# Macaron kernel: the mixer's carry factors leave GpSimd for ScalarE and VectorE, under a new table of places for all jobs

## What is computed

```python
x = x + 0.5 * ffn(layernorm(x))      # passes q = 0..3, one for each batch
x = x + mixer(layernorm(x))          # mixers b = 0..3
x = x + 0.5 * ffn(layernorm(x))      # passes q = 4..7
```

```python
L = clip(cumsum(-dt in the chunk), -20, 0)
cum_decay = clip(cumsum(L[:, :, -1, :]), -80, 0)
ncd = clip(cum_decay - max(cum_decay), -20, 0)
carries = cumsum(shifted(bout * exp(-ncd))) * exp(ncd)
final = chunk_out + carries * exp(L)
```

## Time and profile before

| | before |
|---|---|
| median of 3 executions | 259.51 us (259.31 to 259.81) |
| the profiled execution | 260.13 us |
| its span in the trace | 258.3 us |
| TensorE busy | 251.7 us, 97% of the span |
| VectorE busy | 211.1 us, 82% |
| ScalarE busy | 195.1 us, 76% |
| GpSimd busy | 82.9 us, 32% |
| granted TensorE clock, mean share of full speed | 0.997 |

### The profile page before, as it was taken

How to read it: one execution, slowest core, us unless ns; L and a number is a source line. 1 busy time by engine, 2 the same in 40 slices (tenths; PEclk the granted TensorE clock), 3 DMA queues, 4 the chain that set the end, 5 groups by cost and what they waited for, 6 DMA issues and landing times.

```text
span 258.3 us, 4609 instructions
## 1 busy us (share of the span) xinstructions
PE 251.7 (97%) x1540; PEld 218.6 (85%) x1540; DVE 211.1 (82%) x536; ACT 195.1 (76%) x236; POOL 82.9 (32%) x90
## 2 busy tenths in 40 slices
PE   7999999999999999999999999999999999999994
PEld 7979999998998979899979999878678687887894
DVE  4656587798589799999999999999999998675712
ACT  1255664866999877968848989999989957979650
POOL 5225306920019700995502957500306002000000
PEclk9999999999999999999999999999999999999998
DMA  6589749855100077430700700700007000570022
GB/s 194 176 255 338 121 81 362 177 221 206 63 0 0 13 94 242 47 38 9 260 0 0 81 4 0 247 0 0 0 4 246 0 0 3 155 229 24 0 84 82
DMA packets 21975, 26.18 MB, mean 101 GB/s; under 512 B 1280, under 2 KB 17152, under 8 KB 21952
## 3 DMA queue, kind: packets, MB, share of 16 engines
...
...
## 4 chain that ended last, share of the span: by engine, by line
PE 91%; ACT 3%; issue 2%; DMA 1%; DVE 1%; POOL 0%; SPq 0%; DVEq 0%; ACTq 0%; POOLq 0%
PE hid_ps L845 32%; PE y_ps L873 28%; PE y_ps L898 10%; PE aux_ps L984 5%; PE aux_ps L940 4%; PE aux_ps L1016 3%; PE aux_ps L1005 3%; PE hid_ps L1023 2%; PE y_ps L917 1%; PE aux_ps L965 1%; ACT hid L639 1%; DMA m_tok<-wpack_dram 1%; ACT late L729 1%; PE y_ps L1028 1%; PE hid_ps L917 1%
## 5 line engine op out<-in xcount | busy, mean ns | idle before, releaser
L845 PE MATMUL hid_ps<-z_hi,w_parts 128*128 128x512 f32 x256 | 83.9, 410 | 0.4 <-ACT w_parts L592 0.4
L873 PEld LDWEIGHTS y_ps<-w_sb,hid 128*128 128x128 f32 x640 | 77.1, 192 | 4.3 <-DMA w_sb<-wpack_dram 0.8
L873 PE MATMUL y_ps<-w_sb,hid 128*128 128x128 f32 x640 | 78.1, 275 | 0.4 <-ACT hid L639 0.4
L639 ACT ACTIVATE hid<-hid_ps,w_sb 128x1024 f32<-128x1024 f32 x56 | 61.8, 1109 | 16.7 <-PE hid_ps L845 16.4
L845 PEld LDWEIGHTS hid_ps<-z_hi,w_parts 128*128 128x128 f32 x256 | 45.2, 189 | 9.5 <-issue 1.4
L845 PE MATMUL hid_ps<-z_lo,w_parts 128*128 128x512 f32 x128 | 40.1, 394 | 0.0
L1223 DVE TENSOR_TENSOR hid_lo<-hid,hid_hi 128x1024 fp32r<-128x1024 f32 x19 | 22.9, 1218 | 7.8 <-ACT hid_hi L646 7.8
L845 PEld LDWEIGHTS hid_ps<-z_lo,w_parts 128*128 128x128 f32 x128 | 24.0, 188 | 5.6
L646 ACT ACTIVATE hid_hi<-hid 128x1024 fp32r<-128x1024 f32 x19 | 19.6, 1054 | 1.3 <-PE y_ps L898 1.2
L486 POOL TENSOR_SCALAR bias_tok<-w_sb,coef 128x128 f32<-128x128 f32 x10 | 7.3, 734 | 39.1 <-DMA w_sb<-wpack_dram 25.2
L1110 DVE TENSOR_SCALAR f_tok<-xt,f_mv,f_rstd 128x128 f32<-128x128 f32 x64 | 17.7, 351 | 2.0 <-POOL f_rstd L464 1.9
...
## 6 DMA issues: line engine op xcount, KB each, us to landing
w_parts<-w_split SPq DMA_DIRECT2D x12, 512.0 KB, 4.1
w_split<-mix_tmp SPq DMA_DIRECT2D x8, 512.0 KB, 4.9
...
xt<-bias_tok POOLq DMA_DIRECT2D x5, 512.0 KB, 6.5
...
xt<-x_dram SPq DMA_DIRECT2D x3, 512.0 KB, 8.4
out_dram<-xt SPq DMA_DIRECT2D x3, 512.0 KB, 3.2
```

The lines of the kernel that those rows point to most:

```text
L639: nc.scalar.activation(hid[:, slot % HBUF, :], hid_ps[:, slot % 2, :], ACT.Gelu, bias=bias).then_inc(hid_ready, 1)
L845: last = nc.tensor.matmul(hid_ps[:, slot % 2, cols], w, z[:, q % 2, cols], start=first, stop=end)
L873: last = nc.tensor.matmul(y_ps[:, cols], hid[:, slot % HBUF, cols], w_sb[:, q % 2, k, W2_AT + f * P:W2_AT + (f + 1) * P], start=t == 0 and ...
```

## The change

GpSimd's three small jobs per mixer are gone. ScalarE takes the exp of the first decays straight from `decay` (a scale of -1 in the instruction), in an instruction of its own; VectorE computes `ncd` and the differences behind its scan of `cumd`. All tables of places are set anew.

```diff
     "dve": {
...
-        "m_scan2": {0: 930, 1: 1266, 2: 1631, 3: 1995},
+        "m_scan2": {0: 956, 1: 1244, 2: 1586, 3: 1992},
...
-            def mixer_carry_steps(b):
-
-                pool.wait_ge(cumd_done, b + 1)
-                if b:
-                    pool.wait_ge(small_exp, b)
-                nc.gpsimd.tensor_scalar(small[:, 0, :], first_of(decay), -1.0, None, ALU.mult).then_inc(first_done, 1)
-                nc.gpsimd.tensor_scalar(ncd[:, :], cumd[:, :], cumd[:, 0:1], DECAY_MAX,
-                                        ALU.subtract, ALU.min).then_inc(ncd_done, 1)
-                pool.wait_ge(ncd_done, b + 1)
-                nc.gpsimd.tensor_tensor(small[:, 1, 1:NCH], ncd[:, 0:NCH - 1], ncd[:, 1:NCH],
-                                        ALU.subtract).then_inc(small_done, 1)
...
                 nc.scalar.activation(alpha[:, :], dstep[:, :], ACT.Exp).then_inc(alpha_exp, 1)
-                act.wait_ge(first_done, b + 1)
+                act.wait_ge(decay_done, b + 1)
+                nc.scalar.activation(small_e[:, 0, :], first_of(decay), ACT.Exp, scale=-1.0).then_inc(first_exp, 1)
                 act.wait_ge(small_done, b + 1)
-                nc.scalar.activation(small_e[:, :, :], small[:, :, :], ACT.Exp).then_inc(small_exp, 1)
+                nc.scalar.activation(small_e[:, 1, :], small[:, :], ACT.Exp).then_inc(small_exp, 1)
...
                 V.tensor_tensor_scan(cumd[:, :], last_of(decay), cum_cap[:, :], 0.0,
                                      ALU.add, ALU.min).then_inc(cumd_done, 1)
+                dve.wait_ge(cumd_done, b + 1)
+                V.tensor_scalar(ncd[:, :], cumd[:, :], cumd[:, 0:1], DECAY_MAX,
+                                ALU.subtract, ALU.min).then_inc(ncd_done, 1)
+                dve.wait_ge(ncd_done, b + 1)
+                if b:
+                    dve.wait_ge(small_exp, b)
+                V.tensor_tensor(small[:, 1:NCH], ncd[:, 0:NCH - 1], ncd[:, 1:NCH],
+                                ALU.subtract).then_inc(small_done, 1)
```

More of the change, by code:

```diff
@@ L50 @@
     "pe": {
[L51 to L58, removed]
@@ L59 @@
-        "y_turn_y": {5: 2206, 6: 2426, 7: 2600},
+        "f_norm": {1: 169, 2: 349, 3: 809, 4: 1129, 5: 1509, 6: 1806, 7: 2166},
+        "f_route": {1: 189, 2: 529, 3: 869, 4: 1169, 5: 1529, 6: 1829, 7: 2186},
+        "m_norm": {0: 509, 1: 829, 2: 1209, 3: 1489},
+        "m_dt": {0: 669, 1: 1029, 2: 1349, 3: 1629},
+        "m_v": {0: 749, 1: 1069, 2: 1409, 3: 1669},
+        "m_gate": {0: 929, 1: 1269, 2: 1589, 3: 1926},
+        "m_heads": {0: 985, 1: 1309, 2: 1606, 3: 2046},
+        "m_out": {0: 992, 1: 1389, 2: 1612, 3: 2066},
@@ L81 @@
[L81 to L89, removed]
@@ L90 @@
-        "m_scan2": {0: 930, 1: 1266, 2: 1631, 3: 1995},
[L91 to L95, removed]
+        "c_proj": {0: 110},
@@ new lines @@
+        "f_route": {1: 330, 2: 576, 3: 884, 4: 1200, 5: 1573, 6: 1845, 7: 2203},
+        "f_split_w1": {1: 339},
+        "f_coef": {1: 528, 2: 687, 3: 974, 4: 1312, 5: 1611, 6: 1901, 7: 2279},
+        "f_bias": {5: 1988, 6: 2150, 7: 2533},
+        "m_stats": {0: 422, 1: 728, 2: 1042, 3: 1362},
+        "m_normalise": {0: 487, 1: 819, 2: 1160, 3: 1481},
+        "m_clip": {0: 536, 1: 862, 2: 1238, 3: 1529},
[3 rows of a table added]
+        "m_silu": {0: 633, 1: 977, 2: 1317, 3: 1619},
+        "m_silu_lo": {0: 656, 1: 993, 2: 1337, 3: 1629},
@@ new lines @@
+        "m_decay": {0: 747, 1: 1079, 2: 1380, 3: 1681},
+        "m_dstep": {0: 787, 1: 1131, 2: 1416, 3: 1824},
+        "m_cos": {0: 800, 1: 1119, 2: 1454, 3: 1773},
+        "m_sin": {0: 810, 1: 1148, 2: 1468, 3: 1832},
+        "m_u": {0: 835, 1: 1186, 2: 1495, 3: 1855},
+        "m_u2": {0: 870, 1: 1203, 2: 1517, 3: 1956},
+        "m_carry": {0: 904, 1: 1142, 2: 1425, 3: 1819},
+        "m_scan": {0: 925, 1: 1218, 2: 1536, 3: 1968},
+        "m_scan2": {0: 956, 1: 1244, 2: 1586, 3: 1992},
@@ L96 @@
+        "m_gated": {0: 984, 1: 1327, 2: 1614, 3: 2061},
+        "m_add": {0: 999, 1: 1406, 2: 1624, 3: 2076},
+        "s_lo": {40: 1739, 41: 1752, 42: 1810, 44: 1884, 45: 1923, 46: 1945, 48: 2052, 49: 2068, 50: 2124,
+            51: 2178, 52: 2191, 53: 2207, 54: 2287, 55: 2304, 56: 2322, 57: 2388, 58: 2420, 59: 2459, 60: 2482},
+        "y_update": {0: 405, 1: 711, 2: 1030, 3: 1348, 4: 1669, 5: 2371, 6: 2516, 7: 2584},
     },
     "act": {
-        "c_split_rest": {0: 19, 1: 60},
-        "c_pre_hi": {0: 170, 1: 180, 2: 190, 3: 300, 4: 413, 5: 448, 6: 456, 7: 464},
@@ L100 @@
[L100 to L114, removed]
+        "c_split_rest": {0: 60, 1: 100},
+        "c_pre_hi": {0: 250, 1: 260, 2: 270, 3: 293, 4: 453, 5: 466, 6: 497, 7: 508},
@@ new lines @@
+        "c_proj_hi": {0: 485},
+        "f_turn": {1: 180, 2: 340, 3: 813, 4: 1133, 5: 1493, 6: 1786, 7: 2150},
+        "f_split_w1": {1: 306},
+        "f_tanh": {1: 491, 2: 586, 3: 944, 4: 1226, 5: 1536, 6: 1866, 7: 2180},
+        "f_split_w2": {5: 1613, 6: 1968, 7: 2300},
+        "m_scale": {0: 502, 1: 826, 2: 1180, 3: 1460},
+        "m_tap": {0: 514, 1: 853, 2: 1213, 3: 1506},
+        "m_silu": {0: 573, 1: 936, 2: 1270, 3: 1552},
+        "m_silu_hi": {0: 620, 1: 952, 2: 1300, 3: 1580},
@@ L117 @@
     },
     "pool": {
[L119 to L123, removed]
+        "f_rstd": {1: 40, 2: 173, 3: 620, 4: 901, 5: 1449, 6: 1518, 7: 1812},
+        "f_bias": {0: 293, 1: 559, 2: 691, 3: 1049, 4: 1315},
+        "m_rms": {0: 452, 1: 757, 2: 1067, 3: 1381},
@@ L233, in macaron_kernel @@
         dt_t, decay, alpha, u = (mix_tmp[:, i, :] for i in range(PRE_BUF))
-        small = sb("small", [P, 2, NCH])
+        small = sb("small", [P, NCH])
         small_e = sb("small_e", [P, 2, NCH])
@@ L549, in _ @@
                     mixer_affine(b)
-                for b in placed(tick, at["m_carry"]):
-                    mixer_carry_steps(b)
         @block.scalar
```

48 lines of the change are left out of this document (24 added, 24 removed), and 6 rows, old and new, of the table AT.

## The result

The changed kernel takes 261.44 us (median of 5 runs, 261.08 to 261.85); the kernel before takes 259.36 in the same measurement (5 runs, 259.31 to 259.81). The ratio, taken from the single executions and not from the two medians (which would give 1.0080), is 1.0072, with a 95% interval of 1.0057 to 1.0087. The sign and the range of the forecast (260.8 us) held; the loss is 2.08 us by the medians where the sum said 1.34. One execution of all that follow, in e11, ran at a granted clock of 0.563 and took 424.58 us; its ratio leaves it out.

The account below looks back on a forecast made before the run. TensorE's waits were taken to set the time, with VectorE full from `m_gated(0)` to mixer 2's final scan. Loss 2.76 (0.6 + 0.4 + 1.76) less gain 1.42 gave +1.34: median 260.8 us, own range 259.9 to 262.0, overall 259.2 to 262.1.

Parts of the forecast that it names:

- TensorE's own work is unchanged, only waits count: TensorE, busy 251.7 of 258.3 us, keeps its work; the time can move only by what TensorE waits.
- Front 0.3: At `down(0)`: `gelu(0)` no longer stands behind a weight split that waited on a DMA; gain 0.3 us.
- Middle 0.26: At the `down` at 83.05: its gelu no longer stands behind mixer 0's decay block; gain 0.26 us.
- Late 0.86: Between `down(42)` and `down(43)`: nothing stands between `gelu(42)` and `gelu(43)` any more; gain 0.86 us.
- GpSimd's instructions cost nothing before: GpSimd's twelve carry instructions: ScalarE's exp over `small` never waited for them, so removing them gives nothing by itself.
- The added VectorE instructions, 0.22 each: Four added instructions in `m_carry(1)` and `m_carry(2)`: 0.22 us each, 0.88 in all, between 0.6 and 1.2.
- Up to `m_heads(2)`, 0.6 + 0.4 late: VectorE from `m_gated(0)` to mixer 2's final scan: 0.6 us late with hand-over, plus 0.4 new idle time.
- From there to `hid_lo` of slot 40, 1.76: Behind `m_heads(2)`: VectorE needs 16.70 us, TensorE 14.94; loss 1.76, showing at `m_out(2)` and `down(40)`.
- VectorE freed by an idle GpSimd: VectorE, no longer held by GpSimd, keeps up and only the gains stay: 258.1 us; chance 0.13.
- Loss and gain meet: The 0.6 and 0.4 may be nothing and the second stretch lose only 1.4: 259.5 us; chance 0.13.
- ScalarE late as well: `m_silu(3)` ahead of `gelu(38)` delays `down(38)`, or pass 0's bias DMA lands late: another 1 us, 261.8; chance 0.14.

Follow-up runs that it names:

- e11: The kernel before, with the clip of mixers 2 and 3 working on one column instead of 1024: 259.47 us, ratio 1.0001.
- e1: The changed kernel's new bodies (carry work moved off GpSimd) with every place of the old order, against the kernel before: 260.14 us, ratio 1.0021.
- e2: The new order alone, old bodies with GpSimd's carry steps put back into the new table, against the kernel before: 265.83 us, ratio 1.0239.
- e12: The changed kernel with mixer 2's sine product and rotation sum moved behind `f_normalise(5)` on VectorE: 261.63 us, ratio 1.0083.
- e8: The changed kernel with `hid_lo` of slot 40 moved ahead of mixer 3's decay job on VectorE: 262.70 us, ratio 1.0120.
- e5: New order with carry work on GpSimd, mixer 0's carry scan and GpSimd steps moved right behind the difference of the decays: 260.66 us, ratio 1.0053.

## Why the prediction was right, and where it was off

By its own steps:

- **TensorE's own work is unchanged, only waits count.** Right: the sum of waits accounts for all fourteen kernels, to about 0.3 us.
- **Front 0.3.** Right: the wait of 0.53 ahead of `down(0)` is 0.21. `gelu(0)` starts at 13.62, ahead of the 14.1 to 14.3 forecast, but half a microsecond and more of that is the earlier first `up` of this execution (11.79 for 12.44); counted from that `up`, the gelu is 0.34 earlier. **Middle 0.26.** The waits at `up(20)` and `down(19)`, 0.34 together, are gone. New small ones ahead of `m_heads(0)` take part of both back, so the stage gives 0.41 where I had 0.56. **Late 0.86.** Right, no wait at `down(43)`.
- **GpSimd's instructions cost nothing before.** Right for the old order: ScalarE's exp over `small` never waits in the kernel before, and e1 gains nothing. In the new order they cost 5.2 us at one place (e2), which the prediction did not look at: it priced GpSimd's removal at the old places only.
- **The added VectorE instructions, 0.22 each.** A bit low. Timeline of the changed kernel's VectorE:

```profile
145.76 0.22 DVE L1323 TENSOR_TENSOR_SCAN cumd<-mix_tmp,cum_cap 128x32 f32<-128x32 f32 x1
146.02 0.24 DVE L1326 TENSOR_SCALAR ncd<-cumd 128x32 f32<-128x32 f32 x1
146.29 0.19 DVE L1331 TENSOR_TENSOR small<-ncd 128x31 f32<-128x31 f32 x1
146.74 1.65 DVE L1075 BATCH_NORM_STATS2 f_stat<-xt 128x6 f32<-128x128 f32 x8 [0.26 <-issue]
```

  Three small instructions that wait for each other take 0.64 us to the next start in mixer 1, where one took 0.13: 0.51 for two. In mixer 2 it is 0.98, with 0.26 idle behind it. Together 1.35 for my 0.88.
- **Up to `m_heads(2)`, 0.6 + 0.4 late: this term was mis-sized.** It measures 2.03. The mechanism stands: VectorE takes 69.08 us from `m_gated(0)` to the end of the scan, where TensorE's work between the two `m_heads` is 68.25. I had 67.72 and 0.4, 68.12. The window, read as in the earlier trace rows:

```profile
97.00:166.08 69.08, 68.85 (x446) 59.69 (x444) 67.67 (x166) 60.35 (x78) 22.72 (x26) 1.00 0.24 53
```

  The missing 0.96 are the 0.47 of the carry blocks, 0.15 more idle time (1.41 in all), and two jobs longer by 0.29 and 0.26 beside GpSimd's bias steps and the DMA that it issues behind them (below); these are 0.2 too many, since the 0.26 idle behind the carry block of mixer 2 is in the first two. My 0.98 from `m_heads(0)` to `m_gated(0)` was a misreading, the start of one in the chain (95.30) against that of the other in the timeline: by the timelines it is 1.14 in both kernels (95.14 to 96.28, 95.86 to 97.00), which adds 0.16 to the lateness and makes the old margin 1.0, not 1.1. The wait showed in other places than forecast: 0.25 at `m_out(0)`, which now stands right behind `m_heads(0)`, 0.30 at `m_norm(2)`, 0.46 each at `m_norm(3)` and `f_norm(5)`, and at `m_heads(2)` itself TensorE arrives just as the scan ends (166.08, 166.14). That is what e12 turns round.
- **From there to `hid_lo` of slot 40, 1.76.** Measured 1.55 (0.68 at `m_out(2)`, 0.82 at `down(40)`), in the two places named. That ScalarE is only 1.1 us ahead of VectorE there (e8) was not in the sum and didn't have to be.
- **Rivals.** VectorE freed by an idle GpSimd: fell, e1 is slower and its small and large VectorE instructions last as long as before. (VectorE is lengthened at times beside GpSimd, but beside the bias steps, which both kernels have.) Loss and gain meet: no. ScalarE late as well: `gelu(38)` did not hold up `down(38)`, and the bias DMA took 7.2 us to land for 6.5, without a wait.

In sum: 0.41 + 0.86 gained for the forecast 1.42, and 2.03 + 1.55 lost for 2.76, which nets 2.3 by the count of one profile and 2.08 by the medians. Of these, some 0.8 are the moved work and some 1.3 the order (e5).
